# Graph network kernel: each of GpSimd's element writes waits for the write four before it

## What is computed

```python
x = layernorm(x + L0(x))   # three GCN layers: out[d] = sum over edges (h[s] @ W) * dinv[s] * dinv[d] (+ self loops) + b, relu between
x = layernorm(x + L1(x))   # GATv2, 4 heads: softmax over the edges of a node, then a weighted sum
x = layernorm(x + L2(x))   # two SAGE layers: mean over the edges of a node @ Wl + x @ Wr
x = layernorm(x + L3(x))   # two layers, mean over the edges with the roles of src and dst swapped
```

## Time and profile before

| | us |
|---|---|
| median of three runs | 6769.15 (6765.42 to 6769.48) |
| span of the profiled execution | 6773.4 |
| PE busy | 3327.6 (49%) |
| DVE busy | 2834.7 (42%) |
| POOL (GpSimd) busy | 2848.7 (42%) |
| ACT busy | 1678.0 (25%) |

### The profile page before, as it was taken

How to read it: one execution, slowest core, us unless ns; L and a number is a source line. 1 busy time by engine, 2 the same in 40 slices (tenths; PEclk the granted TensorE clock), 3 DMA queues, 4 the chain that set the end, 5 groups by cost and what they waited for, 6 DMA issues and landing times.

```text
span 6773.4 us, 61344 instructions
## 1 busy us (share of the span) xinstructions
PE 3327.6 (49%) x19159; PEld 3101.4 (46%) x19160; DVE 2834.7 (42%) x3813; ACT 1678.0 (25%) x2774; POOL 2848.7 (42%) x2780
## 2 busy tenths in 40 slices
PE   0000000000006999997444444427601999959697
PEld 0000000000005989997333334326601898959697
DVE  7000000000006454545766667679850443444345
ACT  0000000000003545453000000003310554636365
POOL 2776666667770000000677767736787000020200
PEclk9999999999998999998556565558955999979898
DMA  9691000000004858683333333215600754848686
GB/s 364 217 391 60 1 1 1 1 1 1 1 1 141 270 187 275 193 274 117 90 85 86 86 87 89 84 35 169 192 13 18 253 193 147 275 140 282 208 273 199
DMA packets 589168, 931.28 MB, mean 137 GB/s; under 512 B 99379, under 2 KB 359433, under 8 KB 582550
## 3 DMA queue, kind: packets, MB, share of 16 engines
q1 hardware_dynamic: 464722, 701.52, 32.8%
q10 hardware_dynamic: 42484, 162.22, 6.1%
q0 software_dynamic: 81744, 64.83, 4.1%
HBM read 692.69 MB, written 235.58 MB: 137 GB/s over the span
## 4 chain that ended last, share of the span: by engine, by line
PE 35%; another core or an unknown queue 34%; DVE 14%; issue 11%; POOL 2%; ACT 1%; DMA 1%; DVEq 1%; SPq 0%; ACTq 0%; POOLq 0%
PE banks L899 29%; PE banks L822 3%; POOL work L599 2%; DVE work L1496 1%; DVE Z L1391 1%; DVE Z L1394 1%; DVE Z L1396 1%; DVE big L1400 1%; DVE work L1187 1%; ACT X L644 1%; DVE V L1092 1%; DVE Z L1398 1%; DVE Z L1297 1%; DVE V L1093 0%
## 5 line engine op out<-in xcount | busy, mean ns | idle before, releaser
L899 PE MATMUL banks<-wides,rows 128*128 128x384 f32 (+2 forms) x11040 | 2043.2, 346 | 282.4 <-issue 153.9
L899 PEld LDWEIGHTS banks<-wides,rows 128*128 128x128 f32 x11040 | 1957.0, 190 | 363.0 <-issue 178.0
L599 POOL DMA_INDIRECT work<-tab,stage x832 | 896.4, 1077 | 1527.9 <-ACT stage L752 1264.7
L1258 DVE CAST wides<-big 128x768 fp32r<-128x768 f16 (+3 forms) x1429 | 811.6, 569 | 1348.6 <-PE banks L899 1069.8
L674 ACT CAST wides<-big 128x768 fp32r<-128x768 f16 (+2 forms) x1037 | 832.4, 805 | 675.4 <-PE banks L899 563.9
L844 PE MATMUL banks<-work 128*128 128x50 f16 x784 | 93.8, 278 | 1815.9 <-issue 1692.4
L569 POOL DMA_INDIRECT cells_b<-queue_i x784 | 816.2, 1041 | 303.7 <-issue 301.8
L844 PEld LDWEIGHTS banks<-work 128*128 128x128 f16 x784 | 73.2, 149 | 1836.5 <-issue 1710.0
L569 POOL DMA_INDIRECT cells<-queue_i x784 | 767.2, 979 | 319.4 <-issue 312.8
L1186 DVE TENSOR_TENSOR work<-big 128x400 f16<-128x400 f16 x98 | 36.0, 367 | 1814.3 <-remote 1663.0
L953 PE MATMUL banks<-V,work 128*128 x1664 | 368.0, 410 | 413.3 <-ACT work L754 334.0
(11 more groups left out here) (313 smaller groups left out, 3375.6 us busy)
## 6 DMA issues: line engine op xcount, KB each, us to landing
big<-cells SPq DMA_DIRECT2D x490, 416.0 KB
big<-cells SPq DMA_DIRECT2D x441, 384.0 KB
big<-cells_b SPq DMA_DIRECT2D x300, 384.0 KB
cells_b<-work ACTq DMA_DIRECT2D x50, 1600.0 KB
gathered<-work SPq DMA_DIRECT2D x104, 512.0 KB
work<-gathered SPq DMA_DIRECT2D x104, 512.0 KB, 5.0
big<-cells_b SPq DMA_DIRECT2D x100, 416.0 KB
cells<-work ACTq DMA_DIRECT2D x98, 416.0 KB, 14.7
```

The source lines that it names most:

```text
L599: pool.indirect_dma_start(msg[:, j, u, :], None, tab[0][:, :], bass.IndirectOffsetOnAxis(ap=stage[:, j * U + u:j * U + u + 1].bitcast(U32) ...
L899: last = pe.matmul(banks[:, 4 * (w % 2) + j, 0:(z - a) * P], rows2[:, s, part * D:(part + 1) * D], wides[:, q % QUEUE, (a - start) * P:(z ...
L1258: dve.tensor_copy(wides[:, (2 * m + 1) % QUEUE, 0:(z - a) * P], halves[:, m % HALVES, a * P:z * P]).then_inc(s_wided, 1)
```

## The change

Four semaphores for each list instead of two, taken in turn by the writes and not by the pieces. Write n of a list (n = 56 b + u) raises `s_scat[k][n % 4]`, and from n = 4 on it waits first until the write that took this semaphore before, n - 4, has landed. The wait at u = 8 is gone; `s_written` is raised and the next piece fetched at u = 4. The two rows of numbers that SP and GpSimd load into registers (`written`, `zeroed`) are loaded with a check of their bounds while the kernel runs. SP's and GpSimd's waits for the whole of a list are for four semaphores instead of two.

```diff
+AHEAD = 4
...
-        s_scat = [[sem(f"s_scat{k}_{j}") for j in range(2)] for k in range(2)]
+        s_scat = [[sem(f"s_scat{k}_{j}") for j in range(AHEAD)] for k in range(2)]
...
+        def bounded(engine, row, first, n, most):
+            return nc.values_load_multi_w_load_instructions(row[0:1, bass.ds(first, n)], engines=[engine], min_val=0, max_val=most)[1]
+
         EDGES = 16 * 8
         CONSTS = 16
-        SETTLED = 16 * COLS // 2
+        SETTLED = 16 * COLS // AHEAD
...
-            written = registers(mybir.EngineType.SP, ready_i, 0, len(FIRST) - 1, PIECES)
+            written = bounded(mybir.EngineType.SP, ready_i, 0, len(FIRST) - 1, PIECES)
...
                     for u in range(PIECE):
-                        if u == 8:
-                            if b:
-                                pool.wait_ge(s_scat[k][(b - 1) % 2], 16 * PIECE * ((b - 1) // 2 + 1))
-                                if k == 0:
-                                    pool.sem_inc(s_written, 1)
+                        n = b * PIECE + u
+                        if n >= AHEAD:
+                            pool.wait_ge(s_scat[k][n % AHEAD], 16 * (n // AHEAD))
+                        if u == AHEAD:
+                            if b and k == 0:
+                                pool.sem_inc(s_written, 1)
                             if b + 1 < PIECES:
                                 fetch(k, b + 1)
                         pool.indirect_dma_start(to[:, :], bass.IndirectOffsetOnAxis(ap=queue_i[:, b % 2, u:u + 1].bitcast(U32), axis=0),
-                                                queue_i[:, b % 2, PIECE:RECORD].bitcast(H16)[:, u:u + 1], None).then_inc(s_scat[k][b % 2], 16)
+                                                queue_i[:, b % 2, PIECE:RECORD].bitcast(H16)[:, u:u + 1], None).then_inc(s_scat[k][n % AHEAD], 16)
...
-            zeroed = registers(mybir.EngineType.Pool, ready_i, len(FIRST) - 1, PIECES, len(FIRST))
+            zeroed = bounded(mybir.EngineType.Pool, ready_i, len(FIRST) - 1, PIECES, len(FIRST))
```

More of the change, by code:

```diff
@@ L64, in build @@
     assert ROWQ * 256 == NC and DUMP % 256 == 0 and NPAD < 8191 and NC <= 8192 and COLS <= 2048
-    assert sum(FIRST) == CT and sum(SWEEPS) == CT and sum(BACKS) == TILES and COLS % PIECE == 0
+    assert sum(FIRST) == CT and sum(SWEEPS) == CT and sum(BACKS) == TILES and COLS % PIECE == 0 and PIECE % AHEAD == 0
     ctx = ExitStack()
@@ L469, in dense_strips @@
                         else:
-                            for j in range(2):
+                            for j in range(AHEAD):
                                 sp.wait_ge(s_scat[0][j], SETTLED)
```

## The result

The kernel after takes 6569.99 us (median of 4 runs, 6554.09 to 6571.57) against 6767.28 us for the kernel before beside it (4 runs, 6762.36 to 6769.48): a ratio of 0.9706, 95% interval 0.9692 to 0.9720, or 197 us less. The profiled execution of after has a span of 6568.5 us, 204.9 less than the span of before (6773.4). The experiments show a second thing that no profile of this pair could show: the kernel before has another condition in which it takes 5160 us, and there the same change costs 1.3%.

The account below looks back on a forecast made before the run. PE's increments, seen late while GpSimd issues, let the end of GpSimd's writes (2040 us) set the first aggregation's start. Earlier strips give -150 against the profiled 6773.4, 6623, put at 6620 us; range 5850 to 6880.

Parts of the forecast that it names:

- partly freed: Likeliest case: PE in time beside ACT's clears, late again once the engines are quiet; 6620 us (6560 to 6660), chance 0.32.
- Part 2: Writes beside ACT's clears, about 325 to 525 us: the wait blocks, pitch 1.77 us, GpSimd's block ends 47 us later.
- L: Time from the end of a write's issue to its landing: 5.8 us taken beside the clears, at most 1.79 in the quiet.
- the crawl: Stretches where GpSimd issues and PE's semaphore increments are seen late: one step of the counting loop or strip per 22.4 us.
- the rival built on it: Landing takes about 2.0 us everywhere, so no wait ever blocks and time stays 6769 us; chance 0.12.
- Part 3: Counting loop: at pitch 1.77 us PE's increments come in time; loop ends about 430, aggregation 0 begins about 530 instead of 2114.
- Part 4: Aggregations from 530 to 2087 us: late increments return at 525, 69 of 245 strips get done; gain taken as 150 us.
- Part 5: Guard at u = 8 dropped, earlier fetch and `s_written`, bounds checks, SP's two extra waits: all worth nothing.
- Freed throughout: Rival: late increments never return, in the quiet stretches either; 5600 to 5860 us, 5750 taken, chance 0.23.
- No change: Rival: load beside the clears never makes landing exceed 3.8 us, so no wait blocks; 6769 us, chance 0.12.
- much slower: Rival: a blocked wait of GpSimd is itself seen 22 us late; 20 such waits cost +450 us; chance 0.03.
- Slower: Rival: waits block beside the clears but PE's increments stay late, so 47 us delay aggregation 0; 6816 us, chance 0.30.

## Why the prediction was right, and where it wasn't

**What it rests on.** The likeliest case, partly freed, came with all its stages: 6570 against 6620 us, inside its own range (6560 to 6660). The gain is 197 us where 150 were forecast.

**Part 2, where the cap blocks.** Right in size, but the total by luck: two errors cancel. With L = 5.8 I had a pitch of 1.77 and 28 writes in 50 us; there were 28 and 27 (L is 6.1 for the write shown). But I let the cap bind only from 325 us. It binds from 144 us, since ACT's clears of `cells` load the DMA engines just as well; by 450 us 64 writes are missing and not 34. And I let them be caught up at 1.39. Writes alone, first in before, then in after:

```profile
130.00:450.00 320.00, 217.33 (x222) 1.00 0.79 298
650.00:1100.00 450.00, 308.04 (x316) 1.00 0.02 1
```

```profile
130.00:450.00 320.00, 176.69 (x158) 0.81 1.00 389
650.00:1100.00 450.00, 339.96 (x350) 0.52 0.10 26
```

From 650 to 1100 us after makes 34 writes more, at 1.29 us each instead of 1.42. PE is idle there up to 840 us, so nothing can stretch the pitch. It stays short for 250 us more, when the crawl is back, and before did the same: its crawl is on from about 180 us, and GpSimd's count falls from 41 to 36 in 50 us only from 400 us on. So the 1.39 of rows 5 is that of an old crawl; why a young one leaves the pitch alone isn't settled. The block ends at 2086.07, 46 us later than in rows 3; I had 47. The Trainium skill's page "DMA: Bandwidth & Descriptors", section "Anatomy of one DMA" (about 2.0 us for a small one of GpSimd's) holds in the quiet, where not even a cap of 2 blocked; beside 400 GB/s the trace shows 7.08, and the rival built on it fell.

**Part 3, what the pitch does to the crawl.** The mechanism was right, and read from rows 9 alone, 26 and 14 gathers of another loop; the uncapped gathers of 219 to 246 us show it again inside the counting loop. It took hold at once and not from 325 us: the loop is through at 315 instead of 430. That moved nothing, since, as reckoned, four pieces of the list open aggregation 0: 545 us, forecast 530.

**Part 4, what is late next.** Here is the term that was mis-sized. The crawl did not return at 525 but at about 870, because GpSimd's writes take longer beside DVE's widenings (1.22 us at 575.59, pitch 1.52), and that keeps the pitch above the border: the first sweep frees itself. It is DVE's work and not the strips' loads: from 545 to 618 us 47 of 48 writes overlap work of DVE and take 1.21 us in the mean, while from 350 to 450 us, with the DMA engines at 1.00, the 40 writes beside no work of DVE take 0.97. It fits that the second sweep is in time for 11 strips only: its first eight writes take 1.14 us in the mean, at 853 us DVE's widenings pause, the writes are back at 0.97 (857.90) though strips are still being loaded, and from there DVE's waits grow (2.62, 3.69, 5.70 us by 870.08). That the pause is the cause wasn't tested. Then comes a wait that I had left out, 224 us for the eighth piece, which costs little since the crawl would have filled the time with ten strips. By 2075 us 49 + 11 + 52 = 112 strips are done. I had 69, named 106 and 190 us as the case with the first sweep at full pace, and took 150 between the two; aggregation 1 began 192.4 us earlier. A slip in my sum went the other way: the 84 us of rows 8 cover 432 matmuls, which are 54 strips and not 49, so by the same rows 69 strips are worth 107 us and not 115.

**Part 5 and the last four pieces.** Nothing, as forecast: caps of 8 and 14, with all the rest of the change, stand at 1.000. The 12.5 us that came behind aggregation 1 were not forecast; 6.1 of them lie in the gather loop, and those aren't the change's: from first to last gather it takes 1273.0 us before, 1266.9 after, and 1267.2 with the cap of 8, which never binds; 32, 29 and 31 of ACT's waits there end late. The Trainium skill's page "SBUF — State Buffer", section "Who interferes with whom", has DVE and GpSimd block each other for the length of an instruction: the memsets beside DVE (0.85 for 0.48 us) are of that size, the 21.5 us after PE's matmuls are not.

**The rivals.** "Freed throughout" fell: the quiet stretches from 870 us on crawl with the cap in place. Its price was right in kind: a pace of 1.51 us brought 5725 (I had 5750, for a pitch of 1.5 to 1.77). "No change" fell with the landing time, 6.1 us beside the clears, and "much slower" with the 71 waits for a landing at list 0, which idle 79.6 us in all, 1.1 each. "Slower" was wrong for the late condition, but its mechanism, GpSimd's lost microseconds going one to one onto the end, is what the prompt condition shows: list 0 ends 61 us later and the gather loop begins 59 us later there; I had 47.

**What the prediction could not see.** It took the crawl in the trace for a property of the kernel. It is one of two conditions, and the sign of the change hangs on which is met: 0.971 in the late one, 1.013 in the prompt one. What decides between them stays open: it isn't the kernel (before and after each showed both) nor the chip as such (number 10 showed both within four minutes). Of the nine sessions five were late.

## What to carry to other kernels

A stretch in which every engine stands while a semaphore is long due is a condition to be confirmed by a second measurement before anything is tuned for it: this change is a gain of 2.9% or a loss of 1.3%. If it is confirmed, change the pace of the engine that floods and not only the number it may have under way, since a cap acts only where landings are already slow; and measure the price of the pace in the other condition too. And ask of each cap what the capped list gates: where the list sets the end, the cap's microseconds are the kernel's.

## What the hardware showed that I had not expected

- Two conditions of the same program, about 5160 and 6770 us, each steady over all executions of a session.
- In the late one PE's increments hang on GpSimd's pitch between indirect DMAs: late at 1.25 (gathers) and 1.27 (writes), and on while the crawl itself stretches the mean to 1.42; in time at 1.51 and 1.52, even with an estimated four writes under way, while the one or two under way in the quiet go with late increments at 1.27. Where between 1.3 and the 1.46 us of rows 9 the border lies, no run in this condition tells.
- In the same stretches ACT's own DMA issues slow down, from 38 to 15 in 20 us.
- GpSimd's indirect write takes 0.97 us beside DMA engines at a share of 1.00, and 1.21 in the mean beside DVE's widenings.
- The idle 0.30 us between two writes of GpSimd is partly cover: a memset of 0.22 us between them costs 0.09.
- Four writes under way bind as soon as the DMA engines are at a share of 1.0 (a pitch of 1.79 to 1.85 us), two also beside strips' loads at 0.88 (2.1 us), and neither in the quiet.
